# Products of two rounded parts for the turned rows of a fused sixteen-sample network

## The reference, cut to what matters

```python
h = edges(x) ++ (U * s @ Vt)[x_txt]                 # [16, 384, 256]
h = h + attention(norm(h))                          # 16 heads of 16, window of 128 keys
# keep the 288 best-scored rows, pass them through a block, leave the others
s = xn @ w_router; top = top_k(s, 288)
h = h + xn.at[top].set(gelu(xn[top] @ w_block))     # xn = norm(h)
# a linear recurrence over the rows with a circulant state matrix
h = h + (states(xn @ B_w.T) @ C_w.T + D * xn)
# a shared network and two of eight experts for every row
logits = xn @ router_w.T + router_b
h = h + shared(xn) + sum_of_two_experts(xn)         # gelu(x @ w1.T + b1) @ w2.T + b2, 1024 wide
```

## Time and profile before

| | us |
|---|---|
| median of three runs | 2091.02 (2086.0 to 2092.26) |
| the profiled execution | 2075.45 |
| its span on the core | 2073.7 |
| PE busy | 1952.0, 94% of the span |
| DVE busy | 1346.1, 65% |
| ACT busy | 1069.5, 52% |
| POOL busy | 766.6, 37% |

### The profile page before, as it was taken

One profiled execution on the slowest core, in us unless ns is written; L12 is line 12 of the kernel. 1 busy time (PEld: TensorE's weight loads), 2 busy tenths in 40 slices (PEclk: granted clock), 3 DMA queues, 4 the chain that ended last, 5 costly groups with the idle time before them and its releaser, 6 DMA issues.

```text
span 2073.7 us, 45068 instructions
## 1 busy us (share of the span) xinstructions
PE 1952.0 (94%) x13784; PEld 1572.3 (76%) x13864; DVE 1346.1 (65%) x3781; ACT 1069.5 (52%) x2509; POOL 766.6 (37%) x1269
## 2 busy tenths in 40 slices
PE   6789999999999999999999999888999999999997
PEld 5556766667666666676666766666999999999997
DVE  5767777677676676777767767655665555656553
ACT  1545545555455555554555545541555555555553
POOL 4012333324333243232332432305354455555554
PEclk9989999999999999999999999989999999999999
DMA  5222121120211202212112021110442332323222
GB/s 172 59 47 61 33 55 44 40 68 23 56 53 29 69 28 56 59 33 54 43 41 68 23 55 38 30 54 23 130 128 44 46 89 46 89 43 87 47 46 40
DMA packets 81091, 116.56 MB, mean 56 GB/s; under 512 B 20964, under 2 KB 61508, under 8 KB 78724
## 3 DMA queue, kind: packets, MB, share of 16 engines
q1 hardware_dynamic: 54372, 84.16, 14.6%
q0 software_dynamic: 23360, 27.91, 8.2%
q10 hardware_dynamic: 3312, 3.94, 0.7%
HBM read 51.58 MB, written 26.71 MB: 38 GB/s over the span
## 4 chain that ended last, share of the span: by engine, by line
PE 76%; DVE 11%; issue 8%; POOL 2%; ACT 2%; ACTq 1%; DVEq 0%; DMA 0%; POOLq 0%
PE ps L1888 14%; PE ps L1703 8%; PE ps L1716 5%; PE ps L1899 4%; PE ps L1900 4%; PE ps L1901 4%; PE ps L1633 4%; PE ps L1577 4%; PE ps L1652 3%; PE ps L1549 3%; PE ps L1625 3%; PE ps L1640 2%; PE ps L1694 2%; PE ps L1754 2%; PE ps L1689 2%
## 5 line engine op out<-in xcount | busy, mean ns | idle before, releaser
L819 ACT ACTIVATE prob<-ps,mx 128x256 f32<-128x256 f32 (+1 forms) x768 | 293.9, 441 | 206.9 <-DVE mx L1150 198.5
L1150 DVE TENSOR_REDUCE mx<-ps 128x2 f32<-128x512 f32 (+1 forms) x384 | 227.2, 596 | 205.5 <-PE ps L1625 195.7
L931 ACT ACTIVATE hid_hi<-ps,b 128x256 fp32r<-128x256 f32 x408 | 203.4, 498 | 275.9 <-PE ps L1888 275.9
L811 ACT ACTIVATE pT<-ps 128x512 f32<-128x512 f32 (+1 forms) x384 | 204.2, 532 | 134.8 <-PE ps L1633 132.4
L1479 DVE TENSOR_TENSOR hid_lo<-hid_full,hid_hi 128x256 fp32r<-128x256 f32 x408 | 171.3, 426 | 143.8 <-ACT hid_full L934 143.7
L732 POOL DMA_INDIRECT result<-yb,idx_o x102 | 176.6, 1732 | 165.0 <-DVE yb L1496 143.1
L1633 PE MATMUL ps<-ident,prob 128*128 128x128 f32 x1280 | 208.0, 277 | 26.8 <-ACT prob L819 26.8
L1899 PE MATMUL ps<-w_hi,hid_hi 128*128 128x256 f32 x816 | 230.0, 282 | 0.0
L1900 PE MATMUL ps<-w_lo,hid_hi 128*128 128x256 f32 x816 | 225.5, 276 | 0.0
L1901 PE MATMUL ps<-w_hi,hid_lo 128*128 128x256 f32 x816 | 225.3, 276 | 0.0
L1633 PEld LDWEIGHTS ps<-ident,prob 128*128 128x128 f32 x1280 | 160.5, 143 | 64.6 <-ACT prob L819 30.6
(11 more groups left out here) (283 smaller groups left out, 4109.3 us busy)
## 6 DMA issues: line engine op xcount, KB each, us to landing
w_raw<-in_w SPq DMA_DIRECT2D x16, 1024.0 KB, 6.4
xin<-in_x SPq DMA_DIRECT2D x32, 384.0 KB, 3.7
ks<-k_hi SPq DMA_DIRECT2D x256, 48.0 KB, 2.1
qs<-q_hi SPq DMA_DIRECT2D x120, 96.0 KB, 2.1
ks<-k_lo SPq DMA_DIRECT2D x128, 48.0 KB, 2.1
xn_rows<-xc SPq DMA_DIRECT2D x16, 384.0 KB, 2.5
result<-h SPq DMA_DIRECT2D x16, 384.0 KB, 2.6
qs<-q_lo SPq DMA_DIRECT2D x60, 96.0 KB, 2.1
```

What stands on the lines that cost most here:

```text
L811: act.activation(pT[:, u % TB, :, k0:2, :], ps[:, 2 + u % 2, :].rearrange("p (h k q) -> p h k q", h=2, k=2)[:, :, k0:2, :], ACT.Copy).then ...
L819: ins = act.activation(prob[:, s % PB, hh, w], ps[:, s % 2, hh * 2 * P + w.start:(hh + 1) * 2 * P], ACT.Exp, bias=mx[:, s % 2, hh:hh + 1])
L931: act.activation(hid_hi[:, f], ps[:, f % 4, 0:CHUNK], ACT.Gelu_apprx_tanh, bias=b1[half][:, f:f + 1])
L1150: dve.tensor_reduce(mx[:, s % 2], sc, AX_X, ALU.max, negate=True).then_inc(max_done.sem, 1)
```

## The change

All products of the turned rows become products of parts. ACT's copy out of PSUM now writes xcT_hi, rounded to float32r, and DVE writes the rest xcT_lo with a subtraction that reads PSUM (`turned_rests`); PE waits for the rest in place of the copy. Weights are split once: wr, fb, wb, sw1 and rw each get a hi and a lo buffer. wb and sw1 are loaded later, by SP in the first sequence, and rounded there on ACT (`round_shared`) and DVE (`split_shared`).

To make room, the parts of queries and keys share memory with buffers of the chain: q_hi with g, k_hi and k_lo with rot, q_lo with cum, and xcT_lo with st. So who first writes g or rot in a sequence waits until all four `stacked` semaphores have counted that sample's copies.

Some steps move: the third statistics of the chain from slot 21 to 22 on DVE; hb2 on POOL behind the third xc; the logits from slot 28 to 29; two of three tiles of the values from slot 30 to 28; one of the two later products of the values' sum ahead of BLOCK. The masks before and after become two wide buffers with shifted views. The core of the diff:

```diff
-        xcT = room("xcT", [P, KB, T])
+        xcT_hi = room("xcT_hi", [P, KB, T], F32R)
...
+        with ExitStack() as shared:
+            q_hi = shared.enter_context(nc.sbuf_tensor("q_hi", [P, KB, T], F32R))
         g = room("g", [P, NT, D])
+        with ExitStack() as shared:
+            k_hi = shared.enter_context(nc.sbuf_tensor("k_hi", [P, KB, T], F32R))
+            k_lo = shared.enter_context(nc.sbuf_tensor("k_lo", [P, KB, T], F32R))
         rot = room("rot", [P, 4, T])
+        with ExitStack() as shared:
+            q_lo = shared.enter_context(nc.sbuf_tensor("q_lo", [P, KB, T], F32R))
         cum = room("cum", [P, 2, T])
+        with ExitStack() as shared:
+            xcT_lo = shared.enter_context(nc.sbuf_tensor("xcT_lo", [P, KB, T], F32R))
         st = room("st", [P, 2, T])
...
# SP, ahead of the first sequence
+            sp.wait_ge(mats_read.sem, mats_read.at(0, 1))
+            sp.dma_start(wb, t["wb"]).then_inc(sw1_loaded.sem, 16)
+            sp.dma_start(sw1, t["sw1"]).then_inc(sw1_loaded.sem, 16)
...
# POOL, shared_residual
-                pool.wait_ge(h3_ready.sem, h3_ready.at(b, 1))
+                pool.wait_ge(xc_ready.sem, xc_ready.at(b, 3))
...
# ACT
-                act.activation(xcT[:], ps[:, 6:8, 0:T], ACT.Copy).then_inc(xcT_ready.sem, 1)
+                act.activation(xcT_hi[:], ps[:, 6:8, 0:T], ACT.Copy).then_inc(xcT_ready.sem, 1)
...
# ACT, block_outputs(b, 1), ahead of the write of g
+                    for pair in range(PAIRS) if att else ():
+                        act.wait_ge(stacked[pair].sem, stacked[pair].at(b + 1, stacked[pair].per))
...
+            def round_shared():
+                act.wait_ge(sw1_loaded.sem, sw1_loaded.at(0, 32))
+                act.activation(wb_hi[:], wb, ACT.Copy)
+                act.activation(sw1_hi[:], sw1, ACT.Copy).then_inc(sw1_rounded.sem, 1)
...
# DVE
+            def turned_rests(b, n):
+                dve.wait_ge(xcT_ready.sem, xcT_ready.at(b, n + 1))
+                dve.tensor_tensor(xcT_lo[:], ps[:, 6:8, 0:T], xcT_hi[:], ALU.subtract).then_inc(rest_ready.sem, 1)
...
# DVE, keys(b, chained), between k_hi and k_lo
+                if chained:
+                    turned_rests(b - 2, 2)
...
# DVE, sequence
                     if first and s == 1:
                         eigenvalues()
+                        for pair in range(PAIRS):
+                            dve.wait_ge(stacked[pair].sem, stacked[pair].at(b, stacked[pair].per))
...
-                    if chained and s not in LATER:
+                    if chained and att and s == RANK:
+                        for pair in range(PAIRS):
+                            dve.wait_ge(stacked[pair].sem, stacked[pair].at(b, stacked[pair].per))
+                    if chained and s == RANK:
+                        turned_rests(b - 1, 0)
+                    if chained and s == TURN1 + 1:
+                        turned_rests(b - 1, 1)
+                    if chained and s != LAST_STATS:
                         chain(b - 1, s, not att)
...
+                    if first and s == CONV:
+                        split_shared()
...
# PE (block_tile, drive and logits in the same way)
             def up(b, f):
...
-                for k in range(KB):
-                    ins = pe.matmul(ps[:, 6 + f % 2, 0:T], sw1[:, k, f * P:(f + 1) * P], xcT[:, k],
-                                    start=(k == 0), stop=(k == KB - 1))
+                terms = [(w, x, k) for w, x in ((sw1_hi, xcT_hi), (sw1_hi, xcT_lo), (sw1_lo, xcT_hi)) for k in range(KB)]
+                for n, (w, x, k) in enumerate(terms):
+                    ins = pe.matmul(ps[:, 6 + f % 2, 0:T], w[:, k, f * P:(f + 1) * P], x[:, k],
+                                    start=(n == 0), stop=(n == len(terms) - 1))
...
                 if s == BLOCK:
-                    pe.wait_ge(xcT_ready.sem, xcT_ready.at(b, 1))
-                    for k in range(KB):
-                        ins = pe.matmul(ps[:, 7, 0:T], wr_bc[:, k], xcT[:, k], start=(k == 0), stop=(k == KB - 1))
+                    pe.wait_ge(rest_ready.sem, rest_ready.at(b, 1))
+                    terms = [(w, x, k) for w, x in ((wr_hi, xcT_hi), (wr_hi, xcT_lo), (wr_lo, xcT_hi)) for k in range(KB)]
+                    for n, (w, x, k) in enumerate(terms):
+                        ins = pe.matmul(ps[:, 7, 0:T], w[:, k], x[:, k], start=(n == 0), stop=(n == len(terms) - 1))
...
# PE, sequence
+                    if att and s == BLOCK:
+                        values_sum(b, 1, 2)
                     if chained:
                         chain(b - 1, s, head)
...
                     if head and s == UP + 2:
-                        values(b + 1)
+                        values(b + 1, 2, NT)
...
                     if head and s == TURN2:
                         keys(b + 1)
-                    if chained and s == TURN2 + 1:
+                    if head and s == TURN2 + 1:
+                        values(b + 1, 0, 2)
+                    if chained and s == TURN2 + 2:
                         logits(b - 1)
```

More of the change, by code:

```diff
@@ L57 @@
 UPS = {30: (0,), 31: (1,)}
-LATER = (OUT + 2,)
+LAST_STATS = OUT + 3
 UPS_LAST = (2, 3, 4, 5, 6, 7)
@@ L224, in build @@
         dft, idft, b_w, c_wT = (mats[:, n] for n in range(4))
+        sw1 = place[:, 0:KB * F].rearrange("p (k n) -> p k n", k=KB)
         place = place[:, 4 * KB * D:]
@@ L249, in build @@
             xg_lo = room("xg_lo", [P, KB, 2 * P], F32R)
+            b1 = [room(f"b1_{j}", [P, FB]) for j in range(2)]
+            b2_row = [room(f"b2_row{j}", [P, D]) for j in range(2)]
             w1_raw = room("w1_raw", [P, KB, F])
@@ L867, in round_first, with sequence @@
                 act.activation(w2_hi[0][:], w2_raw[:], ACT.Copy).then_inc(hi_ready.sem, 1)
-            def sequence(b, att, late, chain, head, first_weights=False):
+            def round_shared():
+                act.wait_ge(sw1_loaded.sem, sw1_loaded.at(0, 32))
+                act.activation(wb_hi[:], wb, ACT.Copy)
+                act.activation(sw1_hi[:], sw1, ACT.Copy).then_inc(sw1_rounded.sem, 1)
+            def sequence(b, att, late, chain, head, first=False, first_weights=False):
                 for s in range(SLOTS):
+                    if first and s == TURN1:
+                        round_shared()
                     if head and s in (CONV + 2, CONV + 4):
@@ L913, in _ @@
             act.wait_ge(u_gathered.sem, u_gathered.at(0, 16 * (NB - 1)))
-            sequence(0, True, False, False, True)
+            sequence(0, True, False, False, True, first=True)
             act.wait_ge(late_loaded.sem, late_loaded.at(0, NLATE))
@@ L1384, in sequence @@
                     if head and s == UP - 1:
-                        keys(b + 1)
+                        keys(b + 1, chained)
+                    if chained and not head and s == UP - 1:
+                        turned_rests(b - 1, 2)
                     if head and s == UP:
@@ L1426, in _ @@
             normalise_rows(0)
-            keys(0)
+            keys(0, False)
             query_rests(0)
@@ L1590, in keys, with values @@
                 project(b, wk, 2)
-            def values(b):
+            def values(b, first, last):
                 pe.wait_ge(ctx_ready.sem, ctx_ready.at(b, 0))
-                for i in range(NT):
+                for i in range(first, last):
                     if i == 2:
@@ L1692, in block_tile @@
             def block_tile(i):
-                for k in range(KB):
-                    ins = pe.matmul(tile_out(i), xcT[:, k, i * P:(i + 1) * P], wb[:, k],
-                                    start=(k == 0), stop=(k == KB - 1))
+                terms = [(x, w, k) for x, w in ((xcT_hi, wb_hi), (xcT_hi, wb_lo), (xcT_lo, wb_hi)) for k in range(KB)]
+                for n, (x, w, k) in enumerate(terms):
+                    ins = pe.matmul(tile_out(i), x[:, k, i * P:(i + 1) * P], w[:, k],
+                                    start=(n == 0), stop=(n == len(terms) - 1))
                 return ins
@@ L1749, in drive @@
             def drive(b):
-                    pe.wait_ge(xcT_ready.sem, xcT_ready.at(b, 2))
+                    pe.wait_ge(rest_ready.sem, rest_ready.at(b, 2))
+                    terms = [(w, x, k) for w, x in ((fb_hi, xcT_hi), (fb_hi, xcT_lo), (fb_lo, xcT_hi)) for k in range(KB)]
                     for m in range(2):
-                        for k in range(KB):
-                            ins = pe.matmul(ps[:, 6 + m, 0:T], fb[:, k, m * P:(m + 1) * P], xcT[:, k],
-                                            start=(k == 0), stop=(k == KB - 1))
+                        for n, (w, x, k) in enumerate(terms):
+                            ins = pe.matmul(ps[:, 6 + m, 0:T], w[:, k, m * P:(m + 1) * P], x[:, k],
+                                            start=(n == 0), stop=(n == len(terms) - 1))
                     ins.then_inc(u_done.sem, 1)
@@ L1769, in logits @@
             def logits(b):
-                    pe.wait_ge(xcT_ready.sem, xcT_ready.at(b, 3))
```

(10 more changed lines are left out.)

88 lines of the change are left out of this document (54 added, 34 removed).

## The result

The changed kernel takes 2207.1 us (median; 2205.5 to 2207.4) where the kernel before, in the same series, takes 2088.5 (2084.3 to 2092.3): a ratio of 1.0572, 95% interval 1.0551 to 1.0592. **Slower by 118.6 us; 2208 was forecast**, with 2155 to 2250 as the range. The profiled execution took 2207.44 us, span 2205.7.

The account below looks back on a forecast made before the run. PE sets the pace inside the loop. 14 samples at +7.0 us (+98), sample 1 +10.4, sample 0 +10 and the last sequence -1 make +117 us, so 2208 us from the median 2091.02; 8 in 10 range 2155 to 2250.

Parts of the forecast that it names:

- The wait: PE's block starts later because DVE's rest stands behind its wait for SP's 36 copies: +6.3 us a sample (5.8 to 7.0).
- The clock: Behind each stall of PE the clock stays at half for 5.8 us, costing half of that: +2.9 us a sample.
- the products: PE's scores, block tiles and drive get cheaper as float32r products: -1.1 us a sample (-0.7 to -1.5).
- the sum by that rule: With the skill's product times, block and drive save 2.6 instead of 1.1 us; the total is about +95 us.
- The statistics: Statistics moved from slot 21 to 22 and hb2 behind xc shorten the way to the queries: -1.1 us (0 to -1.8).
- sample 0: In the first sequence, DVE's maximum of unit 1 waits for the copies, plus rounding wb and sw1: +10 us (8 to 14).
- sample 1: BLOCK in the second sequence waits for the copies, less 1 us for its cheaper products: +10.4 us.
- the end: Last sequence without attention or wait: two rests (+2) against cheaper products (-3), -1 us.
- A clock that stays up: Rival: PE's clock stays up through the stall, +76 us: 2167 us; chance 0.13.
- A clock that falls back again during the first units: Rival: the clock also falls back there, as in the second sequence, +159 us: 2250 us; chance 0.15.
- the signs named: Signs included a period near 91 us, PE idle ahead of the scores, and slices with a low clock once per sample.
- Copies that are not last: Rival: PE's cheaper products decide instead of SP's copies, -2.4 us a sample, -36 in 15: 2055 us; chance 0.06.

Follow-up runs that it names:

- the order of two steps: Changed kernel with VectorE taking xcT's first rounding rest ahead of its wait for the 36 copies: 2116.6 us, ratio 1.0116.
- the queue of 12 copies: Changed kernel with the queries' 12 of 36 copies issued by ScalarE's queue: 2108.4 us, ratio 1.0079.
- the wait alone: Kernel before with one wait added, ScalarE's copy of the turned rows ahead of the block waiting for the 36 copies: 2214.9 us, ratio 1.0602.
- the dummy products: Changed kernel with 44 products of a zero matrix on PE ahead of the block's wait: 2177.2 us, ratio 1.0408.
- Statistics back: Changed kernel with the chain's last statistics one unit earlier and GpSimd's residual behind the chain's sum again: 2220.7 us, ratio 1.0629.
- the second profile of before: The kernel before, unchanged, profiled once more for its start: span 2089.0 us.
- both cures: Changed kernel with the rest ahead of VectorE's wait and the queries' copies by ScalarE's queue: 2078.8 us, ratio 0.9955.
- the first wait later: As both cures, with VectorE's first-sequence wait for sample 0's copies and the eigenvalues' powers moved to unit 8: 2076.0 us, ratio 0.9945.
- both cures and the statistics back: As both cures, with the statistics and the residual placed as in the kernel before: 2098.9 us, ratio 1.0044.
- the two waits: Kernel before with waits for the copies ahead of the rank work on VectorE and GELU on ScalarE, nothing else: 2118.8 us, ratio 1.0132.

## Why the prediction was right, step by step

**The wait.** +6.3 was forecast, with bounds 5.8 and 7.0; the way from the first copy to the scores grew by 6.46. Its parts: landing 1.75 instead of 1.57 us, rest 0.96 instead of 0.954, SP's issue 22.80 as read. Shown by the order of two steps, by the queue of 12 copies, and by the wait alone.

**The clock and the products.** They were forecast as two terms, +2.9 and -1.1, together +1.8. The clock measured +1.91 by the dummy products (1.87 in the block itself, 5.30 to 3.43 in the mean). What is left of the period, 90.88 - 84.31 - 6.46 + 1.33 - 1.91, is -0.5 for the products. Together +1.4, so the sum was near and both terms were too big. They are not independent: at full clock the block saves 0.69 us (3.98 to 3.29), as sized from the earlier trace rows (-0.65), but behind the wait, where most of the block runs at half clock, it saves little: in the mean of samples 1 to 14 it takes 5.30 us with rounded products and 5.54 with float32 behind the wait alone. Statistics back against the wait alone, 92.21 and 92.17, says it again: as long as the copies are last, the rounded products are worth next to nothing. The size for 384 columns was good: six products of the ups in the loop take 1.046 us, 174 ns each, for the 178 taken; 18 block products take 2.14 us, 119 ns, for 120. Those are the measured numbers against the Trainium skill's "TensorE: Matmul & The Clock Gate", section "Back-to-back issue gap", from which 114 and 98 ns had been estimated: on these products the trace decides against it, and the sum by that rule (+95) would have come out too low.

**The statistics.** -1.1 forecast, -1.33 measured, by the two mechanisms named: PE's stall 1.77 to 0.46 us, xc 2.27 to 1.06.

**The start.** Against the second profile of before, the first sequence's first maximum comes 2.0 us later, its last 12.8 us later: 10.8 for sample 0, where +10 was forecast, of which 6.6 went away when the wait moved. The scores of sample 0 come 24.1 us later, so 11.3 for sample 1 (+10.4). The 14 intervals from there add 91.9 (+98), the end 0.7 (-1). 24.1 + 91.9 + 0.7 = 116.7, where +117 was forecast. That it agrees to the microsecond is luck: the loop was forecast 6 us too long, the start nearly 4 too short (2.0 of them ahead of the first maximum, which had no term) and the end 1.7 too short. The prediction's own range, summed straight from its bounds, is 2189 to 2237 and not 2185 to 2232; the measured time lies in both.

**From which time it starts.** I added the sum to the median, 15.6 us above the first profile; the second profile shows that this was right and most of why: xT starts 11.7 us later.

**The rivals.** A clock that stays up was to give 2167; with dummy products that keep it up it is 2177. A clock that falls back again during the first units: the windows show 1.00 from 802. (Of the signs named, the page's slices are 55 us long here and can't show a low clock once in a sample; the windows do.) Copies that are not last were to give 2055, a sum made of PE's cheaper products and the statistics; with both cures it is 2078.8. The direction was right and the size not. A sample was to save 2.4 us; it saves 1.74 in the mean and some 2.0 where the clock stays full (82.3 against 84.3). And that rival had no term for the start, where sample 0 still waits: the first scores come at 154.10 with both cures and at 139.25 in the second profile of before. That the clock falls behind the logits was in no forecast.

## What to carry to other kernels

A buffer that two steps share costs a wait, and its price is set by what stands behind that wait in the engine's queue, far more than by its length: waits of 7.0 us on VectorE cost 1.76 us a period where only the rank work and GELU stood behind them, and similar ones cost 6.5 or more where PE's next products did. So when memory is shared, put what others wait for ahead of the new wait, and look which queue issues the transfers that it waits for; here each of the two brought back most of the loss, and together all of it. And cheaper products that need an extra step ahead of them are counted with that step: 0.69 us saved in the block, 0.96 us of rest on VectorE ahead of it. A mean period can hide two kinds of samples: look at the intervals one by one, and at the granted clock in each, before a gain is called absent.

## What the runs showed of the hardware that was not expected

The clock fell while PE was busy. In the sample of the changed kernel shown above it was 1.00 through the 18 logits (rounded products of 8 columns), and about 1 us behind them it fell to half, with PE busy all the time; the windows, columns as above:

```profile
773.00:775.50 2.50, 2.47 (x20) 2.28 (x20) 2.47 (x6) 0.00 (x0) 0.00 (x0) 1.00 0.64 157
775.50:779.70 4.20, 4.20 (x17) 3.62 (x16) 3.79 (x25) 2.25 (x3) 0.00 (x0) 0.63 0.47 102
```

It does so in 4 of samples 1 to 14 of the changed kernel, with both cures in 3, with the first wait later in 4, and with both cures and the statistics back in 10. In the kernel before, with 12 float32 instructions of 8 columns at the same place, the clock stays 1.00 from 777 to 787, and it stays 1.00 there in all 14 samples of both profiles of that kernel, of the wait alone and of the two waits. In the changed kernel the fall costs nothing, because that stretch is covered by SP's copies: PE arrives later and stands idle for 5.5 to 6.0 us instead of some 7.1. Once the copies are not last it costs some 1.6 us each time, as the intervals above show. The places differ in more than the kind of the products: there are 18 instead of 12, one slot later, and eight of the twelve products of the values stand ahead of them now. None of these was tried alone, so why the clock falls in these kernels only, and in some samples only, stays open.

And how long the half clock lasts behind a stall is not the same in every sample. In the changed kernel the block took 4.56 us behind a stall of 7.13 us and 5.92 behind one of 7.15 (samples at 705.50 and 432.66); behind the wait alone, with stalls of 6.5 to 7.1 us, the float32 block took 5.39 to 5.72. What a low clock costs is therefore read from all samples of the loop, not from one.
